# The gates' products of a pair of batches as seven block products instead of eight

## The reference, cut to what matters

```python
x_in = jnp.concatenate([x_conv, x_nmp], axis=-1)
gi = x_in @ w_ih.T + b_ih
gh = x @ w_hh.T + b_hh
r = jax.nn.sigmoid(gi_r + gh_r)
z = jax.nn.sigmoid(gi_z + gh_z)
nn_ = jnp.tanh(gi_n + r * gh_n)
return (1.0 - z) * nn_ + z * x
```

## Time and profile before

| | us |
|---|---|
| median of three runs | 1901.02 |
| the profiled execution, whole | 1900.66 |
| its span in the trace | 1898.8 |
| TensorE busy in the span | 1865.0 |
| VectorE busy | 1180.3 |
| ScalarE busy | 1026.5 |
| GpSimd busy | 824.5 |
| mean granted clock of TensorE | 0.997 |

### The profile page before, as it was taken

How to read it: one execution, slowest core, us unless ns; L and a number is a source line. 1 busy time by engine, 2 the same in 40 slices (tenths; PEclk the granted TensorE clock), 3 DMA queues, 4 the chain that set the end, 5 groups by cost and what they waited for, 6 DMA issues and landing times.

```text
span 1898.8 us, 29888 instructions
## 1 busy us (share of the span) xinstructions
PE 1865.0 (98%) x10268; PEld 1635.8 (86%) x10268; DVE 1180.3 (62%) x2251; ACT 1026.5 (54%) x1834; POOL 824.5 (43%) x1054
## 2 busy tenths in 40 slices
PE   5999999999999999999999999999999999999997
PEld 5999999999999989888888888888888888888886
DVE  8898898989887855444464554554455455445544
ACT  5888888888888875545462333233233323323331
POOL 6788888788766743333341221222122122212210
PEclk9999999999999999999999999999999999999999
DMA  6465555656555426656684344434534443454443
GB/s 197 134 203 203 192 192 182 197 172 203 189 195 178 150 101 149 152 139 147 148 238 126 81 101 112 102 87 103 117 79 103 110 103 86 103 117 81 101 103 56
DMA packets 506900, 262.61 MB, mean 138 GB/s; under 512 B 364808, under 2 KB 472712, under 8 KB 504703
## 3 DMA queue, kind: packets, MB, share of 16 engines
q1 hardware_dynamic: 506750, 260.71, 50.0%
HBM read 151.57 MB, written 109.05 MB: 137 GB/s over the span
## 4 chain that ended last, share of the span: by engine, by line
PE 96%; DVE 1%; ACT 1%; issue 0%; DMA 0%; SPq 0%; POOL 0%; DVEq 0%; ACTq 0%; POOLq 0%
PE P L104 78%; PE P L604 5%; PE P L878 5%; PE P L654 4%; PE P L633 3%; PE P L625 1%; DMA st_w<-in_w0t 0%; DMA yt<-y_d 0%; DVE x L445 0%; ACT hdxh L308 0%; DVE sm L434 0%; DVE ah L424 0%; PE P L1276 0%; DVE hdxl L403 0%; DVE ot L995 0%
## 5 line engine op out<-in xcount | busy, mean ns | idle before, releaser
L862 POOL TENSOR_TENSOR xnx1l<-xnf,xnx1h 128x1024 fp32r<-128x1024 f32 x16 | 44.3, 2766 | 350.0 <-ACT xnx1h L855 350.0
L862 POOL TENSOR_TENSOR xnx0l<-xnf,xnx0h 128x1024 fp32r<-128x1024 f32 x15 | 41.5, 2767 | 322.6 <-ACT xnx0h L855 322.6
L960 ACT ACTIVATE tr<-P,cold 128x512 f32<-128x512 f32 x64 | 44.2, 690 | 198.6 <-PE P L104 198.6
L963 ACT ACTIVATE nn<-gn,col 128x512 f32<-128x512 f32 x64 | 46.3, 723 | 179.3 <-DVE gn L977 179.3
L535 POOL TENSOR_TENSOR axl<-af,axh 128x512 fp32r<-128x512 f32 x64 | 83.4, 1304 | 133.9 <-ACT axh L361 133.9
L984 DVE SCALAR_TENSOR_TENSOR tz<-tz,tr 128x512 f32<-128x512 f32 x64 | 44.3, 693 | 152.6 <-ACT tz L967 152.6
L967 ACT ACTIVATE tz<-P,cold 128x512 f32<-128x512 f32 x64 | 44.0, 688 | 164.0 <-PE P L104 164.0
L973 DVE SCALAR_TENSOR_TENSOR gn<-tr,gn 128x512 f32<-128x512 f32 x64 | 43.9, 686 | 126.8 <-ACT tr L960 126.8
L604 PE MATMUL P<-ft,h 128*128 128x240 f32 x512 | 114.3, 366 | 0.6 <-DVE x L445 0.6
L878 PEld LDWEIGHTS P<-gt,yt 128*128 128x128 f32 x768 | 108.3, 191 | 5.4 <-DMA yt<-y_d 0.5
L104 PE MATMUL P<-w1mh,xxh 128*128 128x512 f32 x256 | 112.1, 438 | 0.0
(11 more groups left out here) (218 smaller groups left out, 6713.1 us busy)
## 6 DMA issues: line engine op xcount, KB each, us to landing
...
```

Of the source, the lines that this page charges most:

```text
L862: e.e.tensor_tensor(o[1][:, :, :], xnf[p % 2][:, :, :, :].rearrange("p c i t -> p c (i t)"), o[0][:, :, :], ALU.subtract).then_inc(done, 1)
L963: e.e.activation(nn[:, :], gn[:, :], ACT.Tanh, bias=n_b[:, o:o + 1]).then_inc(S["nn"], 1)
```

## The change

Operand and weight of each product are taken as 2 by 2 blocks: the operand by half of the features and batch of the pair, the weight by half of the features and half of the outputs. Four result blocks (output half o, batch i) then take seven block products instead of eight, made from sums and differences of blocks (the form with shared sums). The seven steps j of a round run one after the other for all three operands (XC, NM, XN), first r and z in one bank (RZ), then both parts of the new value in another (IN), with 256 columns each. Steps 0, 2, 4 and 5 are summed up in one bank, which ScalarE copies out (`snap`) in between; steps 1, 3 and 6 go to banks of their own and are added by VectorE (`add`). Activations therefore read SBUF. The sums of operand blocks are made before the split into high and low parts (`sums_of_blocks`), so there are now three sorts of split parts: `base` (two blocks as they are, steps 0 and 1), the four sums (`tx`, steps 2 to 5) and `last` (step 6). The weights' seven blocks are prepared in the same way during frequencies 30 to 38. The inverse transforms move to banks 6 and 7, behind steps 3 and 4. The gates of half 0 of a pair are worked out in the next round. The core of the diff, without buffers, names and the removed functions:

```diff
+        ws = [third.hl(f"ws{k}", [128, 3, 7, 128]) for k in range(3)]
...
+        XC, NM, XN = range(3)
+        RZ, IN = range(2)
+        BANKS = (0, 1, 0, 2, 0, 0, 2), (3, 4, 3, 5, 3, 3, 5)
+        SUM, HIGH, LOW = ("tc", "tm", "tx"), ("hic", "him", "hix"), ("loc", "lom", "lox")
+        def steps(p, j, g):
+            return 14 * p + 2 * j + g + 1
...
+        def load_weights(e, k):
+            e.wait_ge(S["unit"], 4 * UNITS)
...
+            w_v = wgt[256 * k:256 * k + 256].rearrange("(h p) (g o m) -> h o p g m", h=2, g=3, o=2)
+            for h in range(2):
+                e.e.dma_start(wt[:, :, h, :], w_v[h, 0]).then_inc(S["lwt"], 16)
+                e.e.dma_start(wr[:, h, :, :], w_v[h, 1]).then_inc(S["lwt"], 16)
+        def weights_sums(e, k):
...
+            e.e.tensor_tensor(wt[:, :, 4, :], wt[:, :, 0, :], wr[:, 0, :, :], ALU.subtract)
+            e.e.tensor_tensor(wt[:, :, 3, :], wr[:, 0, :, :], wr[:, 1, :, :], ALU.add).then_inc(S["wsum"], 1)
+            e.wait_ge(S["wsum"], n + 1)
+            e.e.tensor_tensor(wt[:, :, 2, :], wt[:, :, 3, :], wt[:, :, 0, :], ALU.subtract).then_inc(S["wsum"], 1)
+            e.wait_ge(S["wsum"], n + 2)
+            e.e.tensor_tensor(wt[:, :, 6, :], wt[:, :, 1, :], wt[:, :, 2, :], ALU.subtract).then_inc(S["wsum"], 1)
+        def weights_negative(e, k):
+            e.wait_ge(S["lwt"], 64 * (3 - k))
+            e.e.mul(wt[:, :, 5, :], wr[:, 1, :, :], -1.0).then_inc(S["wneg22"], 1)
+        def weights_high(e, k):
+            e.wait_ge(S["wneg22"], 3 - k)
+            e.wait_ge(S["wsum"], 3 * (3 - k))
+            e.e.copy(ws[k][0][:, :, :, :], wt[:, :, :, :]).then_inc(S["whalf"], 1)
+        def weights_low(e, k):
+            e.wait_ge(S["whalf"], 3 - k)
+            e.e.tensor_tensor(ws[k][1][:, :, :, :], wt[:, :, :, :], ws[k][0][:, :, :, :],
+                              ALU.subtract).then_inc(S["wg"], 1)
...
+        def sums_of_blocks(e, k, p):
+            f, t = source(k, p), tf[k]
+            source_in(e, k, p)
+            e.wait_ge(S[HIGH[k]], 3 * p - 1)
+            e.wait_ge(S[LOW[k]], 3 * p - 1)
+            e.e.tensor_tensor(t[:, 1, :], f[:, 1, :], f[:, 0, :], ALU.subtract)
+            e.e.tensor_tensor(t[:, 2, :], f[:, 3, :], f[:, 1, :], ALU.subtract).then_inc(S[SUM[k]], 1)
+            e.wait_ge(S[SUM[k]], 3 * p + 1)
+            e.e.tensor_tensor(t[:, 0, :], f[:, 3, :], t[:, 1, :], ALU.subtract).then_inc(S[SUM[k]], 1)
+            e.wait_ge(S[SUM[k]], 3 * p + 2)
+            e.e.tensor_tensor(t[:, 3, :], t[:, 0, :], f[:, 2, :], ALU.subtract).then_inc(S[SUM[k]], 1)
+        def base_high(e, k, p):
+            source_in(e, k, p)
+            e.wait_ge(S["step"], steps(p - 1, 1, IN))
+            e.e.copy(base[k][0][:, :, :], source(k, p)[:, 0:3:2, :]).then_inc(S[HIGH[k]], 1)
+        def base_low(e, k, p):
+            e.wait_ge(S[HIGH[k]], 3 * p + 1)
+            e.wait_ge(S["step"], steps(p - 1, 1, IN))
+            e.e.tensor_tensor(base[k][1][:, :, :], source(k, p)[:, 0:3:2, :], base[k][0][:, :, :],
+                              ALU.subtract).then_inc(S[LOW[k]], 1)
+        def last_high(e, k, p):
+            source_in(e, k, p)
+            e.wait_ge(S["step"], steps(p - 1, 6, IN))
+            e.e.copy(last[k][0][:, :], source(k, p)[:, 3, :]).then_inc(S[HIGH[k]], 1)
+        def last_low(e, k, p):
+            e.wait_ge(S[HIGH[k]], 3 * p + 3)
+            e.wait_ge(S["step"], steps(p - 1, 6, IN))
+            e.e.tensor_tensor(last[k][1][:, :], source(k, p)[:, 3, :], last[k][0][:, :],
+                              ALU.subtract).then_inc(S[LOW[k]], 1)
+        def sums_high(e, k, p):
+            e.wait_ge(S[SUM[k]], 3 * p + 3)
+            e.wait_ge(S["step"], steps(p - 1, 5, IN))
+            e.e.copy(tx[k][0][:, :, :], tf[k][:, :, :]).then_inc(S[HIGH[k]], 1)
+        def sums_low(e, k, p):
+            e.wait_ge(S[HIGH[k]], 3 * p + 2)
+            e.wait_ge(S["step"], steps(p - 1, 5, IN))
+            e.e.tensor_tensor(tx[k][1][:, :, :], tf[k][:, :, :], tx[k][0][:, :, :], ALU.subtract).then_inc(S[LOW[k]], 1)
...
         def branch_vector(e, b):
             p, n = b // 2, b % 2
             e.wait_ge(S["idf"], b + 1)
+            source_in(e, XN, p)
+            for name in ("tc", "hic", "loc"):
+                e.wait_ge(S[name], 3 * p)
             for c in range(2):
-                d = e.e.scalar_tensor_tensor(out=t[:, c, :], in0=P[idft_bank(b)][:, c * 256:c * 256 + 256],
-                                             scalar=b2[:, c:c + 1], in1=xnf[p % 2][:, c, n, :],
+                d = e.e.scalar_tensor_tensor(out=xcf[:, 2 * c + n, :], in0=P[idft_bank(b)][:, c * 256:c * 256 + 256],
+                                             scalar=b2[:, c:c + 1], in1=xf[p % 3][:, 2 * c + n, :],
                                              op0=ALU.add, op1=ALU.add)
             d.then_inc(S["xct"], 1)
-            e.wait_ge(S["xchi"], b + 1)
-            e.wait_ge(S["gz"], 2 * (p - 1))
-            e.e.scalar_tensor_tensor(out=o[1][:, :, n, :], in0=t[:, :, :], scalar=0.0, in1=o[0][:, :, n, :],
-                                     op0=ALU.max, op1=ALU.subtract).then_inc(S["xclo"], 1)
         def branch_scalar(e, b):
-            p, n = b // 2, b % 2
+            n = b % 2
             e.wait_ge(S["xct"], b + 1)
-            e.wait_ge(S["gz"], 2 * (p - 1))
-            e.e.activation(xcx[p % 2][0][:, :, n, :], xct[b % 2][:, :, :], ACT.Relu).then_inc(S["xchi"], 1)
...
+        def product(e, p, j, g, kinds, first, end):
+            for k in kinds:
+                n = 3 * p + (1 if j < 2 else 3 if j == 6 else 2)
+                e.wait_ge(S[HIGH[k]], n)
+                e.wait_ge(S[LOW[k]], n)
+                e.wait_ge(S["wg"], 3 - k)
+                if j < 2:
+                    mov = [h[:, j, :] for h in base[k]]
+                elif j == 6:
+                    mov = [h[:, :] for h in last[k]]
+                else:
+                    mov = [h[:, j - 2, :] for h in tx[k]]
+                for half, gate in (((0, 0), (1, 1)) if g == RZ else ((1 if k == XN else 0, 2),)):
+                    begin = first and j in (0, 1, 3) and k == XN and half == (0 if g == RZ else 1)
+                    t = multiply(e.e, mm3([{0: h[:, gate, j, :]} for h in ws[k]], [{0: m} for m in mov],
+                                          P[BANKS[g][j]][:, 256 * half:256 * half + 256], begin,
+                                          end and k == kinds[-1] and j in (1, 5, 6), [(0, 0)]))
+            return t
+        def gates_tensor(e, p, j, g, middle):
+            if j == 0:
+                e.wait_ge(S["snap"], 8 * (p - 1) + 7 + g)
+            elif j == 1:
+                e.wait_ge(S["sums"], 6 * (p - 1) + 1 + g)
+            elif j == 3:
+                e.wait_ge(S["sums"], 6 * (p - 1) + 5 + g)
+            elif j in (2, 4, 5):
+                e.wait_ge(S["snap"], 8 * p + {2: 1, 4: 3, 5: 5}[j] + g)
+            else:
+                e.wait_ge(S["sums"], 6 * p + 3 + g)
+            kinds = (XN, NM, XC)
+            product(e, p, j, g, kinds[:2], True, False)
             middle()
+            product(e, p, j, g, kinds[2:], False, True).then_inc(S["step"], 1)
+        def group(p, g, o):
+            return (grz, gin)[g][p % 2][o]
+        def snap(e, p, n, g):
+            j, o, i = ((0, 0, 0), (2, 0, 1), (4, 1, 1), (5, 1, 0))[n]
+            e.wait_ge(S["step"], steps(p, j, g))
+            e.wait_ge(S["w"], 2 * (p - 1))
+            e.wait_ge(S["e"], 2 * (p - 1))
+            e.e.copy(group(p, g, o)[:, :, i, :], P[BANKS[g][0]][:, :].rearrange("p (h t) -> p h t", h=2)).then_inc(
+                S["snap"], 1)
+        def add(e, p, n, g):
+            j, o, i, copy = ((1, 0, 0, 0), (3, 1, 1, 2), (6, 0, 1, 1))[n]
+            t = group(p, g, o)[:, :, i, :]
+            e.wait_ge(S["step"], steps(p, j, g))
+            e.wait_ge(S["snap"], 8 * p + 2 * copy + g + 1)
+            e.e.tensor_tensor(t, P[BANKS[g][j]][:, :].rearrange("p (h t) -> p h t", h=2), t,
+                              ALU.add).then_inc(S["sums"], 1)
...
+        def gates_scalar(e, p, o):
+            n = turn(p, o)
...
+            e.wait_ge(S["sums"], 6 * p + (6 if o == 0 else 4))
+            e.wait_ge(S["snap"], 8 * p + 8)
+            e.e.activation(wide(rz, 0), wide(rz, 0), ACT.Tanh, scale=0.5, bias=hrz[:, o:o + 1]).then_inc(S["tr"], 1)
+            e.e.activation(wide(gi, 1), wide(gi, 1), ACT.Identity, scale=0.5,
+                           bias=hn_b[:, o:o + 1]).then_inc(S["gn"], 1)
+            e.e.activation(wide(rz, 1), wide(rz, 1), ACT.Tanh, scale=0.5, bias=hrz[:, 2 + o:3 + o]).then_inc(S["tz"], 1)
+        def new_scalar(e, p, o):
+            n = turn(p, o)
             e.wait_ge(S["w"], n + 1)
+            e.wait_ge(S["oo"], n - 1)
+            e.e.activation(nn[n % 2][:, :], wide(group(p, IN, o), 0), ACT.Tanh, bias=n_b[:, o:o + 1]).then_inc(S["nn"], 1)
+        def gates_vector(e, p, o):
...
             e.wait_ge(S["tr"], n + 1)
             e.wait_ge(S["gn"], n + 1)
```

(114 more changed lines are left out.)

306 lines of the change are left out of this document (99 added, 207 removed).

## The result

The changed kernel takes 2079.82 us (median of 4 runs, 2068.64 to 2084.9) against 1900.68 us of the kernel before on the same chip: ratio 1.0935, 95% interval [1.089, 1.098], 179 us slower. The forecast was 2058 us, range 1930 to 2120. The profiled execution took 2080.76 us, its span is 2079.0.

What follows compares the result with a forecast made beforehand. The prediction took a ring of waiting engine queues, lengthened by GpSimd blocking VectorE, as the bound: 32.1 us a round. Rounds +133, edges and tail +7, clock +17 make +157 us on 1900.7: 2058 us, range 1930 to 2120.

Steps and rivals of the forecast that it cites:

- Products: On TensorE, 189 block products a pair take 22.4 us, with 3.2 us of transforms 25.6 us a pair.
- Ring without collisions, 26.55 us: VectorE's and ScalarE's in-order queues wait for each other; nn behind three sums_high makes a round 26.55 us, above TensorE's 25.6.
- Blocking, 2.1 + 3.4 us: GpSimd blocks VectorE's two-input SBUF operations: new_vector starts 2.1 us late, later new_vector and outputs end 3.4 late; round 32.1.
- rival (a): GpSimd collisions stretch VectorE's operations instead of blocking them, and the clock doesn't fall: 1960 us; chance 0.15.
- The clock, 17 us: TensorE's 4.4 us gap before j=5 lowers its clock in half of the rounds: 1.16 us x 15 = 17 us.
- Rival (d): TensorE's clock falls every round at j=5 and again while j=2 waits for XC's low part: 2119 us; chance 0.15.
- SyncE's transfers: The same 23 transfers a round in another order, each a round ahead: 0, bounds 0 and 1 us a round.
- the weights, priced 0 with 9 as the bound: Preparing weight blocks from frequency 31 to 38 lies beside products: 0, or 9 us if nothing covers it.
- round 0: The first round ends 31.7 us after its start, since branch to base_low of XC lack products beside them: +4.0 us.
- the tail: After the last product, new_vector(31, 1) delays the add and the gates and output follow: 11.6 us, +6.4.
- Rival (b): GpSimd's operations slip into VectorE's PSUM reads, transposes or idle times; ring 26.55 us, time 1872 us; chance 0.10.
- The signs: In the rounds: spacing 30 to 34 us, TensorE about 80% busy, named waits, long new_vector and GpSimd operations, clock below 1.00.

Runs made afterwards that it cites:

- run 12: Changed kernel with GpSimd's round work on VectorE except nm's block sums, nm loaded first, branches together behind j=4's snaps, weights' split and last new_vector later: 1866.69 us.
- run 2: Changed kernel with GpSimd's subtractions in the rounds replaced by writes of zero (low parts of x and nm, nm's block sums left out): 1899.32 us.
- run 5: Changed kernel with GpSimd's subtractions in the rounds as zeros and new_scalar(p, 1) ahead of the three sums_high on ScalarE: 1895.68 us.
- run 3: Changed kernel with new_scalar(p, 1) moved ahead of the three sums_high on ScalarE, nothing else: 2050.84 us.
- run 6: Changed kernel with only the low parts of the block sums of x and nm written as zeros on GpSimd: 2001.69 us.
- run 8: Changed kernel with SyncE issuing the load of nm ahead of that of x, nothing left out: 2115.48 us.
- run 1: Changed kernel with 24 extra unread products of 256 columns on TensorE ahead of its wait at j=5: 2053.25 us.

## Why the prediction came out as it did

- **Products.** 25.6 us of TensorE a round; run 12, where nothing else waits, takes 25.76.
- **Ring without collisions, 26.55 us.** 26.88 in run 2, but not for the reason given, so the agreement is luck in part. By the sum ScalarE's nn closed the ring; run 5 puts nn first, takes 1.74 us off VectorE's wait in the second half, and gets 0.15 us. By the trace of run 5 what closed it there was TensorE's own time and its wait for the snap of j=4, which ScalarE makes behind the relu of the branch; run 12 has the snap first, and the wait is gone. In the changed kernel nn does cost: 1.1 us a round (run 3).
- **Blocking, 2.1 + 3.4 us.** The split comes near: 2.55 us for the two `sums_low` (run 6) and 3.44 for the rest (run 2 against 6). But these include the clock, which the prediction priced apart; the lengthened operations alone are 2.2 + 2.2 us. So that 3.44 meets 3.4 is luck. The first victim is right, dl at 2.86 us in the second half. The second is right for e, behind bxl, and wrong for the outputs: it is the block sums of x, behind bml, instead. oo and x2l are hit only when nm comes early (run 8). Operations are blocked, not stretched (2.83 us for one of 0.69), so rival (a), 1960 us, falls. By the Trainium skill, "SBUF — State Buffer", "Who interferes with whom", the second to issue waits for the first; the trace agrees.
- **The clock, 17 us.** Mis-sized: run 1 gives 27 us back and leaves 13 falls. The step that failed is "a fall in half of the rounds", 15 in all, at j=5 alone. The trace has 35 between 1040 and 2040 us, 1.2 a round: 19 at the stop ahead of j=5, which is 2.8 us on the mean and not 4.4, and 16 at the stop in j=2, which was priced at nothing. A fall lasts 3.4 us, in five cases 6.8. The six rounds without one take 29.7 to 31.4 us, the others 33.5 on the mean. Rival (d) had falls at both places, but two a round and at 2.6 us a round.
- **SyncE's transfers, "each a round ahead: 0".** This step failed. `load_xn(p+2)` waits for dl and holds `load_nm(p+1)` behind it, and ScalarE waits 5.8 us (155.7 / 27) for nm. This sets where GpSimd's batch falls, and is worth 36 us (run 8), in favour of the changed kernel; the bounds of 0 and 1 us a round had looked for a loss only.
- **The 23 us between forecast and profile** (2080.8 less 2058) close by stretches, which come to 23.3: the first gate product 1010.76 instead of 1001.79, +9.0 (the weights, priced 0 with 9 as the bound: the bound was right); round 0, 1010.76 to 1048.66, 37.9 us instead of 31.7, +6.2, of which 3.2 are two inverse transforms that the sum forgot (round 0 holds four), 2.0 a wait for ScalarE's snap ahead of j=2, which stands behind L908 and L910 at 2.5 us each, and 1.0 smaller delays; 30 rounds of 32.87 instead of 32.67, +6.2; the last round 24.9 instead of 24.6; the tail, last product's end 2059.8 to x2l's end 2073.0, 13.2 us instead of 11.6, +1.6.
- **Rival (b)** said that GpSimd's work could slip beside VectorE's reads of PSUM. It did not by itself. Run 12 puts a quarter of it there by hand, 2.9 of 11.6 us, and gives the rest to VectorE; that its 1867 us lie near the rival's 1872 confirms nothing.
- **The signs.** Rounds of 30 to 34 us, TensorE's two waits, dl over 1.5 us, the wait for nn and a clock below 1.00 are all there. TensorE is busy 86% and not 80. GpSimd takes over 1.0 us for 256 elements only in last2l (1.13 us); its other such operations take 0.73 to 0.88.
- **A slip.** 1 us either side of 32.1 is 30 us either side of 2058, so 2028 to 2088 and not 2010 to 2100. The measured time lies in both.
